# First stage of a latent-attention kernel in another order, with one unit's maxima fewer ahead of the body

## The reference, cut to what matters

```python
xn = layernorm(x)                                  # x: 8 x 1024 x 256
q = xn @ Wq                                        # 16 heads of 64
latent = xn @ Wkv_down                             # 64 columns, shared by all heads
k, v = latent @ Wk_up, latent @ Wv_up
attn = softmax(causal(q k^T / sqrt(64)))           # per head
out = x + (attn v) @ Wout + tanh(xn @ weight @ aux1 @ aux2 + bias)
```

## Time and profile before

| | us |
|---|---|
| median of 3 runs | 2234.5 |
| lowest and highest run | 2229.15, 2241.65 |
| the profiled execution | 2230.46 |
| its span, first to last instruction | 2228.7 |
| start of the body in it | 78.06 |

### The profile page before, as it was taken

One profiled execution on the slowest core, in us unless ns is written; L12 is line 12 of the kernel. 1 busy time (PEld: TensorE's weight loads), 2 busy tenths in 40 slices (PEclk: granted clock), 3 DMA queues, 4 the chain that ended last, 5 costly groups with the idle time before them and its releaser, 6 DMA issues.

```text
span 2228.7 us, 31554 instructions
## 1 busy us (share of the span) xinstructions
PE 2125.8 (95%) x9400; PEld 1305.9 (59%) x9400; DVE 1503.1 (67%) x3695; ACT 1091.8 (49%) x1970; POOL 1315.1 (59%) x1163
## 2 busy tenths in 40 slices
PE   6999999999999999999999999999999999999997
PEld 4565565655666555665656556565566555566553
DVE  4667657776577676776667766767658676576662
ACT  3445554554545545455445554455455545445443
POOL 0365665656666566665566655665655666556674
PEclk8999999999999999999999999999999999999999
DMA  3011111111111111111011111111111110111111
GB/s 103 17 33 49 32 44 47 35 45 31 44 42 38 47 35 41 40 53 35 30 44 39 49 39 39 42 37 51 30 44 42 39 49 28 44 47 34 30 32 36
DMA packets 66740, 91.12 MB, mean 41 GB/s; under 512 B 12049, under 2 KB 33425, under 8 KB 66577
## 3 DMA queue, kind: packets, MB, share of 16 engines
q1 hardware_dynamic: 66576, 89.11, 14.3%
HBM read 45.55 MB, written 8.91 MB: 24 GB/s over the span
## 4 chain that ended last, share of the span: by engine, by line
PE 77%; DVE 10%; DMA 4%; issue 2%; ACT 2%; SPq 1%; ACTq 0%; DVEq 0%
PE ps L855 21%; PE ps L869 11%; PE ps L838 11%; PE ps L841 10%; PE ps L809 9%; PE ps L902 9%; PE ps L892 4%; DVE ps L1081 2%; DMA norm<-recips 2%; DVE maxima L1086 2%; DVE xn L1163 1%; ACT q_hi L1057 1%; DVE rows L1098 1%; DMA recips<-rows 1%; DVE norm L1104 1%
## 5 line engine op out<-in xcount | busy, mean ns | idle before, releaser
L1216 POOL TENSOR_TENSOR p_sum<-p_sum,probs 128x512 f32<-128x512 f32 x672 | 864.4, 1308 | 347.0 <-ACT probs L999 345.6
L999 ACT ACTIVATE probs<-ps 128x512 f32<-128x512 f32 x1152 | 673.8, 596 | 576.8 <-PE ps L841 544.5
L1081 DVE CUSTOM_DVE_ANT_0 ps<-ps,causal 128x256 f32<-128x256 f32 (+3 forms) x1024 | 496.4, 503 | 264.1 <-PE ps L869 255.7
L855 PE MATMUL ps<-probs,latent 128*64 128x512 f32 x2304 | 549.5, 604 | 0.0
L838 PE MATMUL ps<-q_hi,k_hilo 128*128 128x512 f32 x1152 | 511.8, 444 | 14.2 <-ACT probs L999 9.9
L869 PE MATMUL ps<-k_hilo,q_hi 128*128 128x512 f32 (+3 forms) x1536 | 480.1, 372 | 14.9 <-DVE maxima L1081 7.4
L1086 DVE TENSOR_REDUCE maxima<-ps 128x1 f32<-128x512 f32 x512 | 352.0, 687 | 197.1 <-PE ps L869 195.2
L841 PE MATMUL ps<-q_lo,k_ones 65*128 65x512 f32 x1152 | 459.3, 399 | 0.0
L869 PEld LDWEIGHTS ps<-k_hilo,q_hi 128*128 128x128 f32 x1536 | 282.1, 191 | 210.6 <-issue 106.3
L1204 POOL TENSOR_SCALAR_AFFINE_SELECT probs<-probs 128x512 f32<-128x512 f32 x256 | 166.3, 654 | 391.8 <-ACT probs L999 389.9
L1216 POOL TENSOR_TENSOR p_sum<-probs 128x512 f32<-128x512 f32 x224 | 286.7, 1294 | 152.1 <-ACT probs L999 150.6
(11 more groups left out here) (91 smaller groups left out, 1592.2 us busy)
## 6 DMA issues: line engine op xcount, KB each, us to landing
q_hi<-q_hi SPq DMA_DIRECT2D x256, 128.0 KB, 2.3
norm<-recips SPq DMA_DIRECT2D x256, 128.0 KB, 2.8
x_in<-in_L_attn_x_bld SPq DMA_DIRECT2D x8, 1024.0 KB, 5.9
out_x<-acc SPq DMA_DIRECT2D x64, 128.0 KB, 1.7
q_lo<-rows SPq DMA_DIRECT2D x128, 4.0 KB
rows<-norm SPq DMA_DIRECT2D x128, 4.0 KB
recips<-rows SPq DMA_DIRECT2D x128, 4.0 KB
probs<-in_L_attn_Wq SPq DMA_DIRECT2D x1, 1024.0 KB, 8.1
```

The costliest lines, as they stand in the source:

```text
L855: last = nc.tensor.matmul(y_bank[g * LATENT:(g + 1) * LATENT, :], latent[par][:, key_block(unit, s), :], probs[:, t % PT_SLOTS, g * BANK:( ...
L999: nc.scalar.activation(probs[:, t % PT_SLOTS, g * BANK:(g + 1) * BANK], st_bank[(2 * t + g) % ST_BANKS], ACT.Exp).then_inc(exp_done, 1)
L1081: nc.vector.tensor_tensor_reduce(bank, bank, causal[:, BANK - w:BANK], 1.0, LOWEST, ALU.add, ALU.max, maxima[:, unit % 4, h:h + 1]).then_i ...
L1216: nc.gpsimd.tensor_tensor(sums, other, probs[:, slot, part], ALU.add).then_inc(pool_done, 1)
```

## The change

The first list is reordered. The work called "constants" is split in "casts" (ahead of the chain `LN3`) and "residuals" (behind the first half of `LN4`), and TensorE waits for them only at the first K. The transposes of Wk go behind the first two transposes of x. The folding of `wqk` is cut in two parts, one ahead of the K projections and one among them and the key transposes. All four x residuals come behind all x transposes. Each q residual comes behind the next Q, and the last one among the first unit's maxima. The turning of the other weights waits for all but two residuals, and one of its banks is 7 instead of 0. `AHEAD` is 1: the second unit's maxima and its row leave the first list, the folding of `wff` follows that of `wvo` directly, and the body's list starts at unit 1.

```diff
-AHEAD = 2
+AHEAD = 1
@@ first_plan
     plan = [("LN0", (0, k)) for k in range(4)]
-    plan += [("LN1", 0), ("LN2", 0), ("W", "constants"), ("LN3", 0)]
+    plan += [("LN1", 0), ("LN2", 0), ("W", "casts"), ("LN3", 0)]
     plan += [("LN4", (0, k)) for k in range(2)]
-    plan += [("W", "turn wq"), ("T", (0, 0, 0)), ("T", (0, 1, 0)), ("W", "fold wqk")]
+    plan += [("W", "turn wq"), ("W", "residuals"), ("T", (0, 0, 0)), ("T", (0, 1, 0)),
+             ("W", "turn wk")]
     plan += [("LN4", (0, k)) for k in range(2, 4)]
-    plan += [("TL", (0, 0, 0)), ("TL", (0, 1, 0))]
-    for c in range(2):
-        plan += [("T", (0, c, 1)), ("TL", (0, c, 1))]
-    for k in range(2):
-        plan += two_parts("K", (0, k)) + [("KL", (0, k))]
-    plan.append(("KN", 0))
+    plan += [("T", (0, c, 1)) for c in range(2)]
+    plan += [("TL", (0, c, half)) for half in range(2) for c in range(2)]
+    plan += [("W", "fold wqk 0"), *two_parts("K", (0, 0)), ("KL", (0, 0))]
+    plan += [*two_parts("K", (0, 1)), ("KL", (0, 1)), ("W", "fold wqk 1"), ("KN", 0)]
     for j in range(PAIRS):
-        plan += two_parts("Q", (0, j)) + [("QL", (0, j))]
-    maxima = [[("MAX", c) for c in max_chunks(u)] for u in range(AHEAD)]
-    return (plan + [("W", "turn others")] + maxima[0] + [("W", "fold wvo"), ("MT", 0)] + maxima[1]
-            + [("W", "fold wff"), ("MT", 1)])
+        plan += two_parts("Q", (0, j)) + [("QL", (0, j - 1))] * (j > 0)
+    maxima = [("MAX", c) for u in range(AHEAD) for c in max_chunks(u)]
+    return (plan + [("W", "turn others")] + maxima[:2] + [("QL", (0, PAIRS - 1))] + maxima[2:]
+            + [("W", "fold wvo"), ("W", "fold wff")] + [("MT", u) for u in range(AHEAD)])
@@ fold_on_pe
-            if what == "constants":
+            if what == "turn wq":
                 pe.wait_ge(consts_made, 7)
-                pe.wait_ge(w_split, CONSTANTS)
...
             elif what == "turn others":
-                pe.wait_ge(p0_free, p0_uses)
+                pe.wait_ge(p0_free, p0_uses - 2)
...
             elif what == "fold wvo":
                 pe.wait_ge(w_copied, 12)
+                pe.wait_ge(p0_free, p0_uses - 1)
...
             elif what == "fold wff":
-                pe.wait_ge(w_copied, 14)
+                pe.wait_ge(w_copied, 15)
@@ tensor_program
                     if kind == "K0":
+                        if count.has("W", "residuals"):
+                            pe.wait_ge(w_split, CONSTANTS)
```

## The result

The changed kernel takes 2459.0 us (median of 4 runs, 2451 to 2486) against 2236.7 for the kernel before on the same chips: a ratio of 1.102, interval 1.092 to 1.111. It is slower by 10%, where 2220 was forecast and 2272 was the upper end. The profiled execution took 2451.6, its span is 2449.9.

The account below looks back on a forecast made before the run. The body was taken as bound by the amount of TensorE's work (97% busy). 2230.5 - 19.9 (first stage) + 4 (moved products) + 5.5 (blocked units) = 2220 us; own range of this case 2210 to 2229, overall range 2208 to 2272.

Parts of the forecast that it names:

- The first stage: Work ahead of the body: reordering gains 19.9 us, so the body starts near 58 instead of 78.
- The moved products: The second unit's 16 products for maxima, moved into the body, cost TensorE 4 us with their transpose.
- The mechanism in the body: With AHEAD at 1, late maxima block scores at every block 4 to 7, 57 units beyond those already blocked.
- The step that reads the planner's constant: AHEAD in the planner: maxima due 4 steps ahead of scores instead of 12; a block b needs b+1 steps' worth.
- the prediction's signs: In the body: ScalarE's and POOL's idle near 10 us; block-7 maxima no longer ending over 10 us ahead of scores.
- The price of one block: Blocked units in the body: 0.1 us a unit, so 6 in all, as ready work fills TensorE.
- the row chosen as nearest: Block-7 unit at the fourth batch's start: TensorE busy 12.00 of 12 us, giving the lower end, 0.
- the upper end: A block 7 of the second octet: 13.5 us long, 12.1 of TensorE work, 1.4 idle, say 2 at most.
- Rival C: Each blocked unit in the body leaves a 1.35 gap and a slow-clock stretch, 3 us a unit: 2390; chance 0.05.
- The bracket: Whole kernel: range 2208 (stage gain 24, blocks free) to 2272 (the middle of B, TensorE running out of filling work).
- The break-even: Blocked units in the body: from 0.28 us a unit the gain of the first stage is gone.

Follow-up runs that it names:

- due_restored: The changed kernel with the due steps of the maxima counted from -8 instead of 0, a lead of 12 steps: 2215.1 us, ratio 0.992 to the kernel before.
- before_due_late: The kernel before with the due steps of the maxima counted from 8 instead of 0, all else untouched: 2433.4 us.
- the run with urgent maxima: The changed kernel with maxima of the unit whose scores come next placed ahead of everything else while its row is missing: 2387.9 us.
- lead8: The changed kernel with the maxima due 8 steps ahead of their scores (initial=-4): 2214.0 us, ratio 0.992 to the kernel before.
- lead14: The changed kernel with the maxima due 14 steps ahead of their scores (initial=-10): 2210.1 us, ratio 0.989 to the kernel before.

## Why the prediction was wrong, point by point

**The first stage was right.** 19.9 us laid out, 20.0 measured. That it came within 0.1 is partly luck, for parts of it erred in both directions: the first folding began at 17.9 instead of 18.75, the K projections, the first of them at half the clock, took 4.2 instead of 2.8, and the Q projections, at a mean clock of 0.77 where 0.67 was kept, took 7.3 instead of 8.4.

**The moved products were right or too dear.** 4 us for the 16 products; the body of `due_restored` is 2 longer than before.

**The mechanism in the body was right.** The step that reads the planner's constant (8 of 12 steps of lead are taken, blocks 4 to 7 are blocked) holds, and `due_restored` and `before_due_late` show it in both directions. Of the prediction's signs for it two are there and one is not: POOL's idle time ahead of the first mask of a block-7 unit is 14.0 us (median, 2.2 before), and the maxima no longer end over 10 us ahead of the scores, but ScalarE's longest idle ahead of an exponential is 5.9 and not near 10. The step also missed units: blocks of 3 have longer gaps too (7.3 against 5.1), which makes 80 units and not 57.

**The price of one block was wrong, and this term decided.** "I take 0.1 a unit, near the rows, so 6": the loss is 241 us over 80 units, 3.0 each where 0.1 was put. Three things failed in this step.

First, the row chosen as nearest. The earlier trace rows show TensorE full at a unit whose scores came 3.2 us behind the last ones (896.3 to 899.5). The new gaps are 7 to 15 us long (medians by block). The lead of 8 steps shows that the row itself was honest: block-7 gaps of 3.2 to 9.5 us cost nothing there. It was a row of another size. That ready work covers the first microseconds of a gap and is then used up fits these runs; no run tests it by itself.

Second, the upper end. The count for one block gave 13.5 us long and 12.1 of work. The traced gap of unit 29, a block 6, is 15.3 long with 11.3 of work in its 15.0 us: 3.7 idle where 1.4 had been counted for a block 7. The work was counted well; the length was short, at least in part by what the list puts ahead of maxima (the run with urgent maxima: 71 us in all). A difference of two near numbers was taken for a bound, and then a tenth of it for the value.

Third, the clock. Rival C, a gap of 1.35 at each unit with a slow stretch behind it, gave 3 a unit and 2390, nearer than any other case, and had 0.05. The trace of before showed only isolated falls, so the chance was set by how rare they were in a kernel without gaps. In the changed kernel they are four times as long, 191 us against 48. The Trainium skill's rule in TensorE: Matmul & The Clock Gate, section "HAM oscillation — how this bites in real kernels", spoke against this change. The trace agrees as far as the clock did fall more often, in 37 stretches of the body against 10. That C's 3 a unit is what was measured is luck: it took 1.7 of the 3 for the clock, and the clock can have cost at most 70 us, 0.9 a unit.

**The bracket was open above.** The break-even stood in the text: 0.28 us a unit undoes the gain, against a counted 1.4 at a block of 7. With a gain of 16 and a term of 57 units times something between 0 and 3, the sum was all in that term; the likeliest case should have stood nearer to 1 a unit, and the range should have reached 2390. Even that range would have missed 2459.

**What stays open.** The loss of 241 splits only roughly: about 70 by the order within a block, about 70 by VectorE's pace with an order that fits, at most 70 by the clock, and these overlap, since the time at 1.2 GHz falls with each of the first two. The row's way adds next to nothing at the margin. No single part, taken away, brings the kernel back; the lead does.

**A version that beats both.** `due_restored`, `lead8` and `lead14` take 2215, 2214 and 2210, 0.8 to 1.1% below the kernel before. Their intervals lie wholly under 1 and overlap, so all three are shown to be faster, and none to be the best of them.

## What to carry to other kernels

A constant that says how much work is done ahead may also set where a queue of due work starts. Before moving it, work out for each consumer when its last input is due against when it is wanted; if that turns negative for the largest consumers, the order itself blocks them at every turn. And price a recurring stall from a row of the same length: here the order with 12 gaps of over 7 us lost nothing that could be seen, the one with 36 lost 115 us and the one with 71 lost 241. A short one that was free bounds nothing.

## What the runs showed of the hardware

TensorE's busy time rose by 149 us with no product added (160 in the body, less in the first stage). Up to 70 of it is the slower clock. The rest comes from the drawing: a product is drawn 0.4 us long and neighbours start 0.23 apart. In a stretch where products are spread out the gaps vanish in the drawing: 13.12 of 15.00 busy with 11.3 of work. Products per microsecond (4.30 before, 3.86 after) showed the loss, and so did doubling the maxima's products: 193 us in one kernel, 59 in the other.

The half clock came without long idle. The longest gap of TensorE inside the changed kernel's body, ahead of its last products, was 3.6 us, and only a dozen were over 1.5, yet 191 us were spent at 1.2 GHz, against 48 before. With the maxima's products doubled, and so with fewer empty places between them, it was 53.
